# A four-layer macaron network on one core: a fifth place for the experts' weights, eight copies given to ScalarE, and a new written order for twenty slots

## The reference

```python
def _L2_ffn_ref(x, router_w, router_b, w1, b1, w2, b2):     # DIM 128, HIDDEN 512, E 8
    logits = jnp.einsum('bsd,de->bse', x, router_w) + router_b
    probs = jax.nn.softmax(logits, axis=-1)
    top1 = jnp.argmax(probs, axis=-1)
    out = jnp.zeros_like(x)
    for i in range(E):
        h = jnp.einsum('bsd,df->bsf', x, w1[i]) + b1[i]
        a, g = jnp.split(h, 2, axis=-1)
        y = jnp.einsum('bsh,hd->bsd', a * jax.nn.sigmoid(g), w2[i]) + b2[i]
        out = out + jnp.where((top1 == i)[..., None], y, 0.0)
    return out
```

## Time and profile before

| | |
|---|---|
| median of 3 runs | 3220.77 us (3209.05 to 3223.18) |
| the profiled execution | 3222.13 us |
| its span in the trace | 3220.3 us |
| mean granted PE clock | 0.894 of full |
| busy: PE, PEld, DVE, ACT, POOL | 84%, 53%, 70%, 53%, 26% |

### The profile page before, as it was taken

The page is one execution under the profiler, slowest core; times in us unless marked ns, Lnnn a source line. Parts: engine busy times, 40 slices in busy tenths (PEclk is TensorE's granted clock), DMA queues, the critical chain, the costliest instruction groups (busy, mean ns, idle before and its releaser), DMA issues.

```text
span 3220.3 us, 64240 instructions
## 1 busy us (share of the span) xinstructions
...
## 2 busy tenths in 40 slices
...
GB/s 104 219 38 66 65 51 1 1 1 1 1 1 1 1 1 1 1 125 247 188 54 2 122 229 202 42 21 21 26 16 3 1 1 1 24 16 26 16 33 10
DMA packets 136844, 159.38 MB, mean 49 GB/s; under 512 B 84949, under 2 KB 111829, under 8 KB 135002
## 3 DMA queue, kind: packets, MB, share of 16 engines
...
## 4 chain that ended last, share of the span: by engine, by line
PE 49%; DVE 23%; ACT 8%; issue 5%; POOL 4%; DMA 3%; SPq 2%; POOLq 0%; DVEq 0%; ACTq 0%
DVE nm L1181 5%; PE ps L1915 4%; PE ps L1140 4%; PE ps L529 3%; PE ps L2117 3%; PE ps L1117 3%; PE ps L1081 3%; PE ps L2283 3%; ACT hand L494 2%; PE ps L387 2%; DMA hand<-in_experts 2%; PE ps L602 2%; PE ps L266 2%; PE ps L2420 2%; PE ps L1900 1%
## 5 line engine op out<-in xcount | busy, mean ns | idle before, releaser
L1181 DVE TENSOR_REDUCE nm<-ps 128x2 f32<-128x256 f32 (+2 forms) x704 | 428.5, 644 | 104.3 <-PE ps L1081 50.2
L1230 ACT ACTIVATE core<-ps 128x512 f32<-128x512 f32 x672 | 360.8, 588 | 100.4 <-PE ps L1122 61.4
L2189 POOL TENSOR_TENSOR pre<-pre,sin 128x512 f32<-128x512 f32 x128 | 236.9, 1871 | 251.7 <-ACT pre L2160 211.0
L328 POOL TENSOR_TENSOR rstd<-ve,weights 128x4 f32<-128x4 f32 x80 | 81.0, 1013 | 843.1 <-DVE ve L305 839.2
L1081 PE MATMUL ps<-hand 128*128 128x128 bf16 (+4 forms) x993 | 239.4, 319 | 46.9 <-DVE nm L1181 42.1
L494 ACT COPY hand<-ps 64x512 bf16<-64x512 bf16 x320 | 185.5, 580 | 152.0 <-PE ps L529 95.3
L1117 PE MATMUL ps<-hand 128*128 128x128 bf16 (+4 forms) x996 | 213.4, 305 | 9.6 <-ACT hand L494 5.4
L1915 PE MATMUL ps<-hand 128*128 128x128 f32 x1408 | 197.4, 300 | 25.5 <-DMA hand<-in_experts 25.4
L2194 POOL TENSOR_TENSOR ss<-ss,weights 128x16 f32<-128x16 f32 x64 | 199.2, 3112 | 72.9 <-DVE ss L2209 71.1
L2323 ACT ACTIVATE core<-ps,nm 128x128 f32<-128x128 f32 x512 | 182.1, 376 | 64.8 <-DVE nm L2340 64.3
L1915 PEld LDWEIGHTS ps<-hand 128*128 128x128 f32 x1408 | 188.1, 215 | 35.3 <-DMA hand<-in_experts 29.3
...
## 6 DMA issues: line engine op xcount, KB each, us to landing
...
core<-shear SPq DMA_DIRECT2D x256, 32.0 KB, 1.9
...
```

The costliest lines, as they stand in the source:

```text
L1181: nc.vector.tensor_reduce(nm_of(unit), src, AX.X, ALU.max, negate=True).then_inc(negmax, 1)
L1230: nc.scalar.activation(prob8[:, i % PROBS, 0:w], m.ps[:, RING[at % NR], 0:w], ACT.Exp).then_inc(ring_out, 1)
L2189: ins = nc.gpsimd.tensor_tensor(o[:, :, :, z:z + hl], x[:, :, :, y0:y0 + hl], sn[:, t, :, z:z + hl].unsqueeze(2).to_broadcast([P, 2, LH, h ...
```

## The change

Three edits.

**1. A fifth place.** `PLACES` becomes 5. The first four places stay where they were; the fifth is a stretch of `m.core`, the buffer with the core's own intermediates. `xs` keeps its offset. SP starts five loads at the slot's start, and `load(i + 5)` follows the store of tile i.

**2. Copies of turned q and k.** `turn_stacks` gets the argument `on_vector`, the pairs that DVE copies. For the second layer-1 feed-forward (l == 1) and batches 2 and 3 it is empty: ScalarE copies all eight pairs of units 22 and 23, whose pre runs in slots 21 and 22.

**3. The order of slots 20 to 39.** The strings of these slots in `ORDERS` are new; others are only wrapped differently.

```diff
-PLACES = 4
+PLACES = 5
...
-def turn_stacks(nc, m, lane, a, stkk, ready, cleared=None, once=False):
+def turn_stacks(nc, m, lane, a, stkk, ready, cleared=None, once=False, on_vector=(1, 3, 5, 7)):
...
     def scalar(act):
-        for pair in range(0, 8, 2):
-            yield 2.0 * pair + 0.8
-            take(act, nc.scalar.copy, pair)
+        for pair in range(8):
+            if pair not in on_vector:
+                yield 2.0 * pair + 0.8
+                take(act, nc.scalar.copy, pair)
 
     def vector(dve):
-        for pair in range(1, 8, 2):
+        for pair in on_vector:
             yield 2.0 * pair + 0.8
             take(dve, nc.vector.tensor_copy, pair)
...
-    turn_stacks(nc, m, lane, a, s.stkk, stacked, cleared)
+    turn_stacks(nc, m, lane, a, s.stkk, stacked, cleared, on_vector=() if l == 1 and b >= 2 else (1, 3, 5, 7))
...
-    {"tensor": "a7b1a2b1a6b1a7b3",
-     "vector": "a2b2a1b1c1b1a2b3a1b2a1b2a1b4a4",
...
+    {"tensor": "b2a6b1a14b1a1b1a1b1",
+     "vector": "b4a1b1a1b6a2b3a1b1a1c1a6",
...
-        m.ring = [hands[1].whole[:, i * EXPERT:(i + 1) * EXPERT] for i in range(PLACES)]
+        m.ring = [hands[1].whole[:, i * EXPERT:(i + 1) * EXPERT] for i in range(PLACES - 1)]
         for a in hands:
-            a.xs = a.whole[:, PLACES * EXPERT:PLACES * EXPERT + TILES * P]
+            a.xs = a.whole[:, (PLACES - 1) * EXPERT:(PLACES - 1) * EXPERT + TILES * P]
```

More of the change, by code:

```diff
@@ L557, in turn_stacks @@
     lane.pairs = pairs
-    lane.add(17.0, tensor=tensor, scalar=scalar, vector=vector)
+    if on_vector:
+        lane.add(17.0, tensor=tensor, scalar=scalar, vector=vector)
+    else:
+        lane.add(17.0, tensor=tensor, scalar=scalar)
     return lane.taken, f + 8
@@ new lines @@
+    {"tensor": "a2c1a2b1a1b1a3c1b1a3c1a9c1a1c1a2b1a3b1a1c1b1a1",
+     "vector": "b3a2b1a3c1b1a1b6a1c1a1b4a8c3",
+     "scalar": "b2a11c1a2b1a3b1a1b1a1",
+     "gpsimd": "b1a2b1a2d1"},
+    {"tensor": "c3b1c1b1a2b1a8c1a8b1a1b1a1c1a2b1",
+     "vector": "b2c1b1c1b1c1b7a2c1b2a1b1a1b1a7c1a1",
+     "scalar": "b2a9b1c1a2b2",
+     "gpsimd": "b2d1",
+     "sync": "a7b1a5"},
+    {"tensor": "b2a7b1a13b1a1b1a1b1",
+     "vector": "b7a1c1a1b2a1b2a1b3a1b1a7",
+     "scalar": "b2a11b3",
+     "gpsimd": "d1b1c1b1",
+     "sync": "a7b1a5"},
@@ new lines @@
+    {"tensor": "b2a2b1a16b1a1b1a1b1a2",
+     "vector": "b11c1a2b2a1b1a1b1a8",
+     "scalar": "b2a9b1a1b1a1b1",
+     "gpsimd": "d1b1c1b1",
+     "sync": "a7b1a5"},
+    {"tensor": "b3a1b1a1b1a2b1a2b1a1b1a1b1a1b1a1b1a2b1a1b1a1b1a1b1a1b1a2b1a1b1a1b1a1b1a1b1",
+     "vector": "b7a1c1a1b2a1b1a1b1a1b2a1b2a1b1a1b1a1b2a1b2a2",
+     "scalar": "b3a1b1a1b1a1b2a1b2a1b1a1b2a1b2a1b1a1b1a1b2a1b3",
+     "gpsimd": "b1c1b4d1b8",
+     "sync": "a9b1a3"},
+    {"tensor": "b1a1b3a1b1a1b2a1b1a1b4a1b2a1b3a1b2a3b2",
+     "vector": "b5a1b2a1b1a1b1a1b3a1b2a1b2a1b3a1b1a1b1a2c1",
+     "scalar": "b3a1b1a1b2a2b5a1b1a1b4a1b1a1b1a2b3",
+     "gpsimd": "b1c1b9d1b3"},
```

185 lines of the change are left out of this document (80 added, 105 removed).

## The result

The median fell from 3216.26 us (20 runs, 3200.24 to 3227.11) to 3201.41 us (20 runs, from 3188.13): a ratio of 0.9959, with a 95% interval from 0.9946 to 0.9972, so 13 to 15 us faster. One of the 20 runs of the changed kernel took 3514.85 us at a mean granted clock of 0.691, and the ratio is taken without it. Forecast were 32 us. The time lies inside the range, but the gain is less than half of the forecast.

The account below looks back on a forecast made before the run. Experts' slots were taken as held by weight waits, the gather and the next unit's late pre. Gains of 19.3 and 13 us sum to -32.3 on 3222.1: 3189.8, or 3188 against the median; range 3150 to 3217.

Parts of the forecast that it names:

- under 12: Sign: PE's waits for weights ahead of the hidden matmuls fall from 25.4 us to under 12.
- near 14: Sign for slot 34: first gated product near 14 us after the last `keep`, held by the gather.
- each alone meets the other's bound: Slots 25, 26, 33, 34: fifth place and new order costed together, 31.5 us at most, 19.3 left after costs.
- Cost 1.4 in each of the three: Slots 26, 33, 34: next pre's front delays the first gated product to 9.4 us where weights allow 8.0.
- The others keep their start; a fifth place takes their share: Slots 24, 27, 32, 35: 4 us gained in 27, 3 in each other from fewer weight waits, together 13.
- I take 0: Attention slots 20 to 23, 28 to 31, 36 to 39: new order gives 0, within -12 to +12 us; ScalarE's copies also 0.
- The floor of 45.7 us for a slot: Experts' slots with no wait but the start: 5.8 + 29.5 + 4.1 + 3.1 + 3.2 = 45.7 us.
- only part is paid: Rival, chance 0.17: the weights' waits go, but the pre's chain still sets the experts' slots; 3203 us.
- More loads in flight each land later: Rival of no change, chance 0.12: with five loads in flight landings reach 11 us, pace 3.6 a tile; 3215 to 3225.
- the 52 us that were named as a sign of being wrong: Sign: the prediction is wrong if the experts' slots stay above 52 us.
- Slower: Rival, chance 0.07: the new order costs 5 us in each of twelve attention slots, +60 against -32; 3249 us.
- What ACT_TABLE_LOAD costs: ScalarE table switches: a 1.38 us drain each would cost three slots up to 2.8 us more each, giving 3196.

Follow-up runs that it names:

- E1: The changed kernel with all order strings and the copies of turned q and k as before, leaving the fifth place alone; ratio 0.9958.
- E4: The changed kernel with the next pre's gates and softmax behind two tiles in slots 25, 26, 33, 34, and slot 34's gather add too; ratio 0.9946.
- E8: Five places, new strings in the experts' slots alone, otherwise as before the change, with gates behind two tiles in slots 25 and 26; ratio 0.9954.
- E14: E8 with 16 added identity matmuls on PE ahead of the transposes in slots 25, 26, 33 and 34; ratio 0.9931.
- E13: The changed kernel with 16 added identity matmuls in PE's wait for the norm in slots 25, 26, 33 and 34; ratio 0.9916.
- E2: The changed kernel with four places again, all new order strings and ScalarE's copies kept; ratio 1.0001.
- E15: E13 with the strings and copies of before in slots 20 to 23, 28 to 31 and 36 to 39; ratio 0.9917.

## Why the prediction was wrong

Part of the mechanism was right: five places take PE's waits for weights from 25.4 to 3.3 us ("under 12"), bn_stats of the next pre starts 0.6 us after the last `keep`, and slot 34 starts with the gather's wait, its first gated product 14.7 us after the last `keep` ("near 14"). The step "each alone meets the other's bound" was not: in slots 25, 26, 33 and 34 the place alone takes 12.4 us, both edits 13.7, and the late pre, which I took for the second bound of slot 26, leaves that slot at 48.8 us in E1. And three terms of the sum were mis-sized.

**The front of the next pre ahead of the first tile: nothing in slot 25, "Cost 1.4 in each of the three" in 26, 33 and 34.** Slot 25 was left out because the softmax stands behind two tiles there. But PE's transposes and gate matmuls stand ahead of its first tile as in the others, and its first gated product came 13.3 us after the last `keep`, where weights allow 8.0. The slot took 51.1 us instead of 45.7, which is 5.4 of the 8.7 us by which the four slots missed their forecast of 195.0. With the gates behind two tiles it takes 44.1 to 45.7 us (E4, E8, and E14 with the added matmuls), against 51.1 to 51.7 in the six traces with the gates ahead and nothing added.

In the other three the chain was added up from durations at full clock, as 9.4 us. It starts with a wait of 3.8 us in which PE has nothing to do, and behind that wait transposes, gates and the first tile ran at less than full clock. Slot 33, where PE waits for no weights at the start, shows the term by itself: the first gated product came at 12.7 us, so the term was 4.7, not 1.4. In slot 26 it came at 13.8, where the weights, landing 8.3 us after their issue, came late as well; E13 shows that there the front at full speed brings nothing forward. The rows for the clock were there: 3.38 us for a tile behind an 8.22 us wait, which I charged for two tiles a slot as if it were a thing of the weights' waits, and didn't ask where PE would wait in the new order. The matmuls of E13 in that wait take off some 10 us (11.6 by the two traces alone).

**"The others keep their start; a fifth place takes their share", -13.** Slots 24, 27, 32 and 35 went from 227.3 to 224.0 us, -3.3. Slot 27 gave 8.2, twice what was said; the other three, from which 9 were to come, grew by 4.9. Slots 24 and 32, where the new order puts more of the next pre ahead, grew by 3.4 and 2.7; slot 24 does so in each of the eleven other traces with its new string (65.0 to 67.8 us, against 62.4 to 63.2 in five with the old), and has slot 25 shorter for it.

**"I take 0" for the twelve attention slots.** Slots 21 to 23 are 5.2 us longer in these two traces, and over all of them 230.1 to 232.0 against 223.6 to 225.6; 28 to 31 are the same (178.9 and 178.7), 36 to 39 grew by 2.3, and slot 20 fell by 2.1. That is 5.2 of the 12 that the bound held; slots 20 to 23 are 1.1% longer, just over the 1% that was said. The named cover for ScalarE's copies, PE's core work, was not enough: PE's idle time rose. How the 6 us are shared between ScalarE alone and the order stays open.

These three make up the miss: 8.7 + 9.7 + 5.2 = 23.6 us over a sum of -32.3, which leaves -8.7 in slots 20 to 39 by issue times, or -11.8 when slots are cut at their ends, where slot 24's late issue counts too. The two spans differ by 20.4, the rest of it in slots whose program is the same; the medians by 14.9.

The floor of 45.7 us for a slot was right for the wrong reason. PE is busy 40 to 46 us in it, not 29.5 + 6.3 + 3.2, as its row already said (43.48); but part of this lies beside the waits that I counted. Slots 33 of the changed kernel and of E13 (46.3 and 46.1) come near it, and slot 25 reaches it or goes under it in E8, E14 and E4 (45.7, 45.2, 44.1).

Of the rivals, "only part is paid" came closest, in amount and not in cause: the pre's chain no longer sets the slots. "More loads in flight each land later" fell with the median landing, 4.7 us into the first four places and 7.8 into the fifth, after 8.0 before; at a slot's start, though, the fifth load takes 10.0 to 13.6 us, where the fourth took 8.9 to 9.9 before. Slot 34 stayed above the 52 us that were named as a sign of being wrong. "Slower" named the right slots and a price of 5 us each; it was 2 us each in slots 21 to 23 (5.2 in three). The rule of the Trainium skill, "ScalarE: Activation LUTs", section "What ACT_TABLE_LOAD costs", by which each switch has a drain beside its load, weighed in the prediction, is not seen on the path: in slot 33 the load back starts 0.02 us behind the exp and takes 1.28, and the first sigmoid starts 1.7 us after its end, held by PE. In slot 25 of E13 two switches stand with nothing to wait for:

```profile
1481.83 1.28 ACT L706 ACT_TABLE_LOAD   x1
1483.12 0.23 ACT L706 ACTIVATE gp<-gl 128x32 f32<-128x32 f32 x1
1483.37 1.28 ACT L1937 ACT_TABLE_LOAD   x1
1484.66 1.14 ACT L1937 ACTIVATE core<-ps,hand 128x128 f32<-128x128 f32 x4
```

From the exp's end to the sigmoid's start are 1.3 us, the load and no more. So the trace does not agree with the page's drain of 1.38 us here, and the rows decide.

What is shown, and what argued: that the place alone gives the gain of the whole change (E1) and the order alone none (E2) is measured, within intervals some 11 us wide. That the gates ahead of the first tile cost slot 25 some 6 us is shown by E4 and E8, and that part of it is the clock behind PE's wait by E13 and E15. That slot 26 starts late because of the load of layer 3's weights is argued from its place and size. Why E1 gains as much as the change although its slots 24 to 27 are 6.7 us longer is by the lengths: its slots 21 to 23 are 7.2 us shorter, 32 to 35 5.6 and 36 to 39 3.9, and slot 20 is 2.1 longer. That the attention slots' loss reaches the time was not shown.
